# Causal attention between two mixture-of-experts layers: the score stage's loop over 16 groups written out, in another order of its pieces

## What is computed

```python
x = x + 0.5 * _L0_ffn_ref(_layernorm(x, axis=-1), ...)
x = x + _L0_attn_ref(_layernorm(x, axis=-1), ...)
x = x + 0.5 * _L0_ffn_ref(_layernorm(x, axis=-1), ...)
# in _L0_attn_ref, after q, k, v are projected and split by head:
scores = jnp.einsum('bqhe,bkhe->bhqk', q, k) * scale
scores = jnp.where(causal[None, None], scores, -jnp.inf)
attn = jax.nn.softmax(scores, axis=-1)
out = jnp.einsum('bhqk,bkhe->bqhe', attn, v)
```

## Time and profile before

| | us |
|---|---|
| median of 3 runs | 1352.32 |
| lowest and highest of them | 1341.02, 1355.78 |
| the profiled execution | 1358.7 |
| its span, first to last instruction | 1357.0 |

### The profile page before, as it was taken

The page is one execution under the profiler, slowest core; times in us unless marked ns, Lnnn a source line. Parts: engine busy times, 40 slices in busy tenths (PEclk is TensorE's granted clock), DMA queues, the critical chain, the costliest instruction groups (busy, mean ns, idle before and its releaser), DMA issues. The chain is left out here.

```text
span 1357.0 us, 39365 instructions
## 1 busy us (share of the span) xinstructions
PE 1159.3 (85%) x14036; PEld 859.3 (63%) x14036; DVE 956.1 (70%) x2205; ACT 772.2 (57%) x1882; POOL 526.6 (39%) x738
## 2 busy tenths in 40 slices
PE   1865999988749979999998999899858689998986
PEld 1655999877538824444444445453846579997875
DVE  7666666557758868788787888792785956664765
ACT  1645666562226616777776787789536456665521
POOL 0643444255614422222332223233426154443564
PEclk9986999989869968999999999999969689998988
DMA  6321444422255661222222222210235034443343
GB/s 209 122 78 55 133 131 132 112 77 74 83 178 167 221 130 47 59 66 61 56 66 56 58 62 59 58 39 3 93 111 158 17 106 133 133 131 92 111 127 104
DMA packets 101001, 132.52 MB, mean 98 GB/s; under 512 B 20253, under 2 KB 85725, under 8 KB 100829
## 3 DMA queue, kind: packets, MB, share of 16 engines
q1 hardware_dynamic: 79324, 86.07, 21.4%
q0 software_dynamic: 13056, 35.67, 9.6%
q10 hardware_dynamic: 8448, 8.39, 1.8%
HBM read 81.35 MB, written 48.23 MB: 95 GB/s over the span
## 5 line engine op out<-in xcount | busy, mean ns | idle before, releaser
L1775 ACT ACTIVATE s_PR<-s_ps_b 128x512 f32<-128x512 f32 (+3 forms) x768 | 323.2, 501 | 126.8 <-PE s_ps_b L1891 123.3
L1796 DVE TENSOR_REDUCE s_MX<-s_ps_a 128x1 f32<-128x512 f32 (+15 forms) x640 | 340.2, 591 | 62.6 <-PE s_ps_a L1867 58.7
L1891 PE MATMUL s_ps_b<-QO,KO 99*32 99x512 bf16 (+3 forms) x3072 | 224.9, 334 | 22.9 <-DMA QO<-s_NMS 17.2
L1746 POOL TENSOR_SCALAR_AFFINE_SELECT s_PR<-s_PR 128x256 f32<-128x256 f32 x256 | 103.1, 408 | 307.5 <-ACT s_PR L1775 306.8
L821 POOL DMA_INDIRECT f_XG<-xn_scratch,f_tok_u x144 | 136.7, 949 | 196.9 <-PE f_ps_x L917 137.7
L1867 PE MATMUL s_ps_a<-KO,QO 96*32 96x512 bf16 (+15 forms) x3072 | 204.4, 329 | 0.6 <-issue 0.6
L1032 POOL DMA_INDIRECT f_YG<-y_scratch,f_slots_u x128 | 127.0, 992 | 120.2 <-DVE X L1143 52.2
L1908 PE MATMUL s_ps_o<-s_PR,s_VG 128*17 128x512 f32 (+3 forms) x1536 | 161.4, 494 | 0.7 <-POOL s_PR L1746 0.3
L1891 PEld LDWEIGHTS s_ps_b<-QO,KO 99*32 99x32 bf16 x3072 | 84.5, 96 | 112.7 <-ACT s_PR L1775 65.7
L927 PE MATMUL f_ps_u<-f_W,f_xh 128*128 x576 | 153.8, 349 | 0.0
L949 PE MATMUL f_ps_y<-f_W,f_hh 112*128 (+1 forms) x576 | 121.1, 303 | 0.6 <-DVE f_hh L881 0.4
(11 more groups left out here) (229 smaller groups left out, 2609.2 us busy)
## 6 DMA issues: line engine op xcount, KB each, us to landing
y_scratch<-f_YS SPq DMA_DIRECT2D x144, 128.0 KB
qk_scratch<-p_QK SPq DMA_DIRECT2D x32, 384.0 KB, 3.1
QO<-qk_scratch SPq DMA_DIRECT2D x96, 128.0 KB, 3.0
KO<-qk_scratch SPq DMA_DIRECT2D x96, 128.0 KB, 2.8
xn_scratch<-f_XN ACTq DMA_DIRECT2D x16, 512.0 KB, 3.8
f_RAW<-in_w_up SPq DMA_DIRECT2D x16, 352.0 KB, 3.2
X<-in_x SPq DMA_DIRECT2D x4, 1024.0 KB, 9.8
x_scratch<-X SPq DMA_DIRECT2D x1, 4096.0 KB
```

Of the source, the lines that this page charges most:

```text
L1746: nc.gpsimd.affine_select(out=tile, in_=tile, compare_op=ALU.is_ge, fill=0.0, base=0, pattern=[[0, 2], [1, P]], channel_multiplier=-1)\
L1775: nc.scalar.activation(PR[:, u // 2 % SLOTS, u % 2, 0:W - lo], ps_b[u % RING][:, lo:W], ACT.Exp, scale=SCALE).then_inc(exp_done, 1)
L1796: nc.vector.tensor_reduce(MX[:, src, s:s + halves, m], ps_a[slot][:, 0:halves * keys].rearrange("p (s n) -> p s n", s=halves), AX.X, ALU.m ...
L1891: last = nc.tensor.matmul(ps_b[u % RING][strip, lo:W], KO[k][0:RM, h, i * P + strip.start:i * P + strip.stop], QO[k][0:RM, h, hf * W + lo: ...
```

## The change

The tables of the order and three places in it are other numbers, and the loop over groups is written out on PE, DVE and ACT. The number of B units, value steps and A units is the same, and so are POOL's and SP's programs. (Of each table the first line is shown.)

```diff
-    A_AFTER = ((0, 0, 2, 0), (3, 1, 0, 0), (0, 1, 1, 1), (1, 1, 0, 2),
+    A_AFTER = ((0, 1, 2, 0), (1, 1, 1, 0), (1, 1, 0, 0), (2, 0, 1, 1),
...
-    V_AFTER = ((0, 0, 0, 1), (1, 0, 0, 1), (0, 0, 0, 0), (1, 0, 0, 0),
+    V_AFTER = ((0, 0, 0, 1), (1, 0, 0, 1), (0, 0, 0, 1), (0, 0, 0, 0),
...
-    OUT_0, OUT_1, MAX_AT = (8, 3), (2, 2), (8, 3)
+    OUT_0, OUT_1, MAX_AT = (8, 1), (3, 2), (8, 1)
...
-            for g, k in steps(act, NG, 4):
+            for g, k in [(n, n % 4) for n in range(NG)]:
...
-            for g, k in steps(dve, NG, 4):
+            for g, k in [(n, n % 4) for n in range(NG)]:
...
-            for g, k in steps(pe, NG, 4):
+            for g, k in [(n, n % 4) for n in range(NG)]:
```

More of the change, by code:

```diff
@@ L1561, in softmax_stage @@
                                      [(1, 1, 1, m) for m in range(NBLK)])
-    A_AFTER = ((0, 0, 2, 0), (3, 1, 0, 0), (0, 1, 1, 1), (1, 1, 0, 2),
-               (0, 2, 0, 1), (2, 1, 0, 1), (0, 2, 1, 0), (1, 2, 1, 2),
-               (1, 0, 0, 0), (1, 0, 1, 0), (0, 3, 2, 0), (0, 1, 1, 1))
-    V_AFTER = ((0, 0, 0, 1), (1, 0, 0, 1), (0, 0, 0, 0), (1, 0, 0, 0),
-               (0, 1, 0, 0), (1, 0, 1, 0), (0, 0, 1, 0), (0, 0, 0, 0),
-               (1, 0, 0, 0), (0, 0, 0, 1), (0, 0, 1, 0), (0, 1, 0, 0))
+    A_AFTER = ((0, 1, 2, 0), (1, 1, 1, 0), (1, 1, 0, 0), (2, 0, 1, 1),
+               (1, 0, 0, 3), (0, 1, 1, 2), (0, 2, 1, 1), (1, 2, 2, 0),
+               (0, 0, 0, 2), (0, 0, 1, 1), (2, 0, 1, 0), (1, 0, 0, 3))
+    V_AFTER = ((0, 0, 0, 1), (1, 0, 0, 1), (0, 0, 0, 1), (0, 0, 0, 0),
+               (0, 1, 0, 1), (0, 0, 1, 0), (0, 0, 0, 0), (1, 0, 0, 1),
+               (0, 0, 0, 0), (0, 1, 0, 0), (0, 1, 0, 0), (1, 0, 0, 0))
     V_LATE = 2
-    OUT_0, OUT_1, MAX_AT = (8, 3), (2, 2), (8, 3)
+    OUT_0, OUT_1, MAX_AT = (8, 1), (3, 2), (8, 1)
     COPY_0, COPY_1 = (4, 3), (1, 0)
```

## The result

The changed kernel takes 1332.28 us, median of 5 runs (1330.48 to 1339.67), against 1355.78 for the kernel before, measured beside it again (1341.02 to 1360.54). The ratio is 0.9855, with a 95% interval from 0.9816 to 0.9894: faster by 1.5%, beyond the 1% that the prediction takes as the least that can be told from no change. (The ratio isn't the quotient of the two medians, which is 0.983; that of the two means is 0.985.) Forecast were 1335 us and a ratio of 0.9867.

What follows compares the result with a forecast made beforehand. PE bounds the score loop, with waits at group ends. Terms of 6.5 + 3.1 + 2.5 + 6.0 = 18.1 us took the profiled 1358.7 to 1340.6, ratio 0.9867; applied to the 1352.3 median: 1334, stated as 1335, range 1324 to 1349.

Steps and rivals of the forecast that it cites:

- term 1: Group ends: PE's value step V7 comes earlier, so SP issues the maxima transfers sooner; 12 waits shrink by 0.54, 6.5 us.
- A landing as long as now: Transfers of the maxima at group ends: landing not shortened, median still 2.9 us, between 1.9 and 3.1.
- POOL in time: POOL's split of the maxima, about 0.9 us later against V7, still doesn't delay the third transfer; 0.6 us left.
- term 2: Jump back of the loop over groups 4 to 11: written out, its 4.02 us wait becomes 0.9, 3.1 us less.
- term 3: Register work inside the loop's groups disappears when written out: 2.5 us, bounds 2 and 6.
- term 4: PE's clock in the score stage: shorter waits remove four of five groups at 0.94; 6.0 us, bounds 0 and 7.5.
- Nothing new stalls: Middle of groups: the new spread of A units doesn't make PE wait for DVE; costed at nothing, otherwise 1.2 us a group.
- The dense stretch: A behind B (4,3) to first A behind (7,2): 16 A units, PE 7.0 us, DVE 8.2; four slots cover 2.0.
- The rival of a stalled fetch: Written-out groups 4 to 11 stall instruction fetch, 8 x 4.1 = 33 us against 12.1: +21, 1373 us; chance 0.08.
- MAX_AT and OUT_0 at nothing: Earlier places of the maxima transpose and output transpose don't decide the transfer wait; priced at nothing.

## Why the prediction was right

The mechanisms were right, in the main. That the number came out so near is in part luck. In groups 0 to 13 of the two traces the four terms are worth some 24.5 us, not 18.1: every one of them was larger than forecast. Parts that no term spoke of took 5.5 us back (2.2 ahead of the stage, 1.5 in group 14, 1.8 behind it), and 19.0 were left.

- **V7 is the gate (term 1).** 6.5 us forecast, 9.8 in the traces. Right, and shown by three runs. The order alone is worth 0.53 us an end (1.15 to 0.62, both written out), where the sum had 0.54. One entry moved back brings 0.45 of it back. And transfers behind V8 make every wait some 2 us longer. The run with SP's call in front of the load fits too, but there the landing is shorter as well. The waits themselves came out at 0.62 and not 0.9. The 0.3 us less appear with the written-out form: the 12 waits other than the back edge's were 1.43 and 1.32 us in the two traces of the kernel before and 0.88 with the new tables looped; the 13 written-out ones were 1.15 with the old tables, 0.62 and 0.63 with the new.
- **A landing as long as now** was term 1's condition, and at one end it doesn't hold. At the end of group 0 PE went on 4.1 us after the third transfer's issue, where it was 3.0 in the kernel before. So this wait grew, from 0.87 (0.99 in the second trace) to 1.48 (1.46), where 0.54 less was forecast. Why is open.
- **POOL in time.** Right: POOL's last piece came 0.07 us before V7's end, and comes 0.80 after it now (645.82 against 645.02), so 0.87 later where 0.9 was forecast. The "some 2.2" in that working is more than its listed pieces, which make 1.75 us.
- **The back edge (term 2).** Right in size for this change: 4.02 became 0.58, 3.4 us against 3.1. The price of the jump by itself was too low, 2.6 against 3.7, which is seen only where nothing else is waited for.
- **The registers (term 3).** 2.5 us forecast, with 6 as the bound. Of the 4 us in these traces some 0.7 are not the loop's: groups written out in both kernels are also 0.05 us shorter. That leaves some 3.3. What the loop costs depends on what stands beside it: 5.7 us over seven groups in the kernel before once the waits are gone, near the bound, but only 1.0 with the new tables and their waits. That only some groups pay was read from rows of one such mixture.
- **The clock (term 4).** 6.0 us forecast, 7.5 seen between these two traces, but the reason was half right. I had a limit between 1.61 and 1.98 us. In the score stage of all these traces no wait under 1.4 us at the end of a group is followed by a stretch at the lower clock. Of seven waits of 1.4 to 1.6 us one is, the one of 1.43. Of eight waits of 1.6 to 1.8 us one is too (1.61), and of twenty of 1.9 to 3.2 us thirteen are. All seven of the latter with the transfers behind V7 are among these; the seven without it are all in the run with the transfers behind V8, up to 3.15 us. Behind the back edge it came each time, in four traces. So shorter waits do remove it, but the length of the one wait doesn't decide alone. With three stretches in its second trace, the kernel before loses 4.5 to 7.5 us by it.
- **Nothing new stalls.** PE doesn't wait for DVE in the middle of groups in the changed kernel. (The dense stretch, counted again from the table, has 15 A units up to the first behind (7,2), not 16.) The rival of a stalled fetch fell too: the written-out kernels have no wait for issue before a B unit.
- **MAX_AT and OUT_0 at nothing.** Right for the transfer, which is what was argued. What was missed is ACT: the two transposes between the second and third B unit keep PE from waiting for a `ps_b` bank, 3.3 us in the trace. The runs don't show a time for it.
- **Missed: group 14.** It got 1.5 us longer. In this group 0.6 come with the new tables (24.2 to 24.3 us besides the wait in all kernels that have them, 23.7 with the old). The rest is the wait at its end. It is at most 0.2 us in the four looped traces, and 0.63 to 1.43 in those written out, but for one of 0.2 (the split between the masks). No term spoke of either.

What stays open is why PE can go on earlier in written-out code. With the new tables, the third transfer of group 4 is issued at the same distance from the start of the exponential of B (8,3) whether looped or not (2.94 us), and PE can go on 4.14 us later in the one trace and 3.20 in the other. At the seven ends inside the loop other than the back edge, the waits are 0.85 us looped and 0.47 and 0.53 written out; at the five ends outside it 0.91, 0.84 and 0.69. So it is seen mostly where the loop was. The page lists queues of instructions among those that the DMA engines serve (1.97 and 0.43 MB before, 1.88 and 0.34 after), and the loop adds register instructions, but no run here separated any of this from chance.

## What to carry over

When an engine waits for a transfer, look at what the issuing queue stood behind, not only at what makes the data. Here the data was ready and the queue waited for a matmul step that had nothing to do with it. One call moved in that queue was worth as much as a new order of three engines and the loss of a loop together. It also put a 128 KB load behind the small transfers, which then landed 0.9 us sooner. Before a hand-written order is tuned further, move the issue out of the way of it; afterwards the old and the new order could not be told apart. A wait can hide other costs beside it (the jump), so what these are worth is read only once it is gone. And moving one piece in a full order can open a stall elsewhere, so read the groups besides the wait too before the time is put down to the piece.

## What the hardware showed

- A runtime loop's jump back stopped PE for 3.7 us when nothing else was waited for, and for 4.0 to 4.5 us at an end where a transfer was awaited too. A group of 25.3 us took 0.56 to 1.1 us more inside the loop when no wait stood at its end.
- PE's clock fell to 1.2 GHz for a stretch that cost 1.5 us (26.96 against 25.42 us busy) behind 13 of 20 waits of 1.9 to 3.2 us, 2 of 15 of 1.4 to 1.8 us, and no shorter one at the end of a group in this stage.
- Transfers of 8 KB each, issued by SP some 0.35 us behind a load of 128 KB, landed 2.8 to 3.0 us after their issue (medians of eight traces, before and changed kernel among them); with no load just ahead of them, after 2.0 or 2.1 us (medians of the four kernels with SP's move). Single ones took up to 4.3 us either way.
